# Two mixture-of-experts blocks: each up-projection from the third expert on as three products of high and low parts

## The reference

```
# layer 0: 8 routed experts, top 2, and one shared expert (a ninth with weight 1)
h = gelu(einsum('bsd,edi->bsei', x, ew1) + eb1)          # 128 -> 512
all_outputs = einsum('bsei,eid->bsed', h, ew2) + eb2     # 512 -> 128
moe_out = einsum('bse,bsed->bsd', weights_E, all_outputs)
# layer 1: 8 experts, top 2, each on its own scaled and shifted rows
normed = xhat[None] * gamma[:, None, :] + beta[:, None, :]
h = relu(einsum('end,edf->enf', normed, W1) + b1[:, None, :])
out = einsum('enf,efd->end', h, W2) + b2[:, None, :] + xf[None]
y = einsum('ne,end->nd', cw, out)
```

## Time and profile before

| | us |
|---|---|
| median of 3 runs | 4264.62 (4262.81 to 4272.31) |
| the profiled execution's own time | 4266.36 |
| its span | 4264.6 |
| PE busy | 4034.6 (95%) |
| DVE busy | 2708.3 (64%) |
| ACT busy | 1815.7 (43%) |
| POOL busy | 2786.1 (65%) |
| one up-projection of an expert on PE | 6.87 |
| one down-projection | 7.14 |

### The profile page before, as it was taken

How to read it: one execution, slowest core, us unless ns; L and a number is a source line. 1 busy time by engine, 2 the same in 40 slices (tenths; PEclk the granted TensorE clock), 3 DMA queues, 4 the chain that set the end, 5 groups by cost and what they waited for, 6 DMA issues and landing times. The chain is left out here.

```text
span 4264.6 us, 71858 instructions
## 1 busy us (share of the span) xinstructions
PE 4034.6 (95%) x26436; PEld 2145.7 (50%) x26436; DVE 2708.3 (64%) x3398; ACT 1815.7 (43%) x2105; POOL 2786.1 (65%) x1342
## 2 busy tenths in 40 slices
PE   7999799999999999999999998899799999999989
PEld 3444355555545545555555545533355554555547
DVE  5666867667676676766767743378667666676542
ACT  3444244444444444444444443246344444444433
POOL 4667087878887787877878891000078878878940
PEclk9999799999999999999999998869899999999989
DMA  1000000000000000000000001100000000000001
GB/s 36 7 6 2 5 2 2 2 2 2 3 2 3 2 2 2 2 3 2 2 1 1 2 1 28 35 1 1 5 2 2 2 2 2 2 1 2 1 13 33
DMA packets 25454, 23.92 MB, mean 6 GB/s; under 512 B 6321, under 2 KB 19106, under 8 KB 25122
## 3 DMA queue, kind: packets, MB, share of 16 engines
q1 hardware_dynamic: 23666, 17.05, 1.4%
q10 hardware_dynamic: 1456, 2.46, 0.2%
HBM read 18.97 MB, written 0.52 MB: 5 GB/s over the span
## 5 line engine op out<-in xcount | busy, mean ns | idle before, releaser
L421 POOL TENSOR_TENSOR c_SUM<-c_SUM,c_PR 128x896 f32<-128x896 f32 (+2 forms) x1170 | 2449.0, 2093 | 463.2 <-ACT c_PR L492 371.4
L588 DVE TENSOR_REDUCE c_MX<-c_XB 128x2 f32<-128x1024 f32 (+2 forms) x1156 | 1391.6, 1204 | 858.5 <-PE c_XB L788 858.3
L492 ACT ACTIVATE c_PR<-c_S 128x1024 f32<-128x1024 f32 (+1 forms) x1224 | 1195.1, 1023 | 1622.9 <-PE c_S L823 1547.2
L841 PE MATMUL c_O<-c_PR,c_V 128*64 128x512 f32 (+1 forms) x4896 | 1179.6, 600 | 0.0
L841 PEld LDWEIGHTS c_O<-c_PR,c_V 128*64 128x64 f32 (+1 forms) x4896 | 317.2, 136 | 540.8 <-issue 418.4
L823 PE MATMUL c_S<-c_SH,c_ONE 64*128 64x512 f32 x2448 | 490.8, 395 | 0.0
L788 PE MATMUL c_XB<-c_KHM,c_QH 64*128 64x512 f32 x1632 | 373.2, 452 | 29.1 <-DVE c_MX L588 20.6
L788 PEld LDWEIGHTS c_XB<-c_KHM,c_QH 64*128 64x128 f32 x1632 | 157.2, 188 | 389.3 <-DVE c_MX L588 211.7
L823 PE MATMUL c_S<-c_QH,c_KHM 64*128 64x512 f32 x1728 | 352.4, 403 | 0.3 <-DVE c_SH L578 0.3
L823 PE MATMUL c_S<-c_QL,c_KHM 64*128 64x512 f32 x1728 | 349.6, 398 | 0.0
L823 PE MATMUL c_S<-c_QH,c_KLM 64*128 64x512 f32 x1728 | 347.6, 397 | 0.0
(11 more groups left out here) (298 smaller groups left out, 4569.4 us busy)
## 6 DMA issues: line engine op xcount, KB each, us to landing
f_W<-in_L_w SPq DMA_DIRECT2D x34, 256.0 KB, 2.7
CTX<-in_ctx ACTq DMA_DIRECT2D x12, 192.0 KB, 4.4
c_WQ<-in_L_xattn_Wq SPq DMA_DIRECT2D x12, 64.0 KB, 1.8
c_WO<-in_L_xattn_Wo SPq DMA_DIRECT2D x12, 64.0 KB, 1.8
c_WK<-in_L_xattn_Wk SPq DMA_DIRECT2D x12, 48.0 KB, 1.7
c_WV<-in_L_xattn_Wv SPq DMA_DIRECT2D x12, 48.0 KB, 1.7
X<-in_x SPq DMA_DIRECT2D x1, 512.0 KB, 6.7
a_WQ<-in_L_attn_Wq SPq DMA_DIRECT2D x8, 64.0 KB, 1.9
```

Of the source, the lines that this page charges most:

```text
L421: pool.tensor_tensor(out[0:kp], out[0:kp], tile[0:kp], ALU.add).then_inc(summed, 1)
L492: act.activation(PR[0:kp, u % BUFS, :, :].rearrange("p h q -> p (h q)"), S[u % 2][0:kp, :], ACT.Exp)\
L588: dve.tensor_reduce(MX[:, q:q + tiles, :, column], bank[:].rearrange("p (h k) -> p h k", h=2) [:, :, 0:tiles * m].rearrange("p h (q k) -> ...
L841: last = pe.matmul(O[ROWS[h], :], V[pair.par][0:kp, t, ROWS[h]], PR[0:kp, u % BUFS, h, :], start=t == 0, stop=t == TILES - 1)
```

## The change

From the third expert of a block on (`e >= 2`; seven experts in `f0`, six in `f1`), `up` makes each unit out of three float32r matmuls that add up in the same bank: high weights by high rows, low weights by high rows, high weights by low rows. The product of the two low parts is left out. ScalarE makes the high parts (`W1H` of each expert's weights; `XEH` of its rows, once for the block in `f0`), VectorE the low parts (`W1L`, `XEL`). The first two experts keep the float32 matmul. Loads and `down` stay as they are.

```diff
+        W1H, W1L = [[sb(f"W1{part}{i}", [P, F], F32R) for i in range(2)] for part in "HL"]
+        several = 2 if normed is not None else 1
+        XEH, XEL = [[sb(f"XE{part}{i}", [P, N], F32R) for i in range(several)] for part in "HL"]
...
                 def up(e, par, ep):
-                    pe.wait_ge(w1_in[par], PER_W * (ep + 1))
-                    if normed is not None:
-                        pe.wait_ge(xe_done, e + 1)
+                    plain = isinstance(e, int) and e < 2
...
+                        terms = [(W1[par], XE[par])]
+                    else:
+                        xh, xl, made = parts(e, par)
+                        pe.wait_ge(w_low, e - 1)
+                        pe.wait_ge(x_low, made)
+                        terms = [(W1H[par], xh), (W1L[par], xh), (W1H[par], xl)]
...
-                            pe.matmul(UP[j % 4][:], W1[par][:, k * P:(k + 1) * P],
-                                      XE[par][:, half * 512:(half + 1) * 512], start=True, stop=True)\
-                              .then_inc(up_done, 1)
+                            for i, (stat, rows) in enumerate(terms):
+                                last = pe.matmul(UP[j % 4][:], stat[:, k * P:(k + 1) * P],
+                                                 rows[:, half * 512:(half + 1) * 512], start=i == 0, stop=i == len(terms) - 1)
+                            last.then_inc(up_done, 1)
...
+                def high_rows(e, par):
...
+                    act.activation(xh[:], XE[par][:], ACT.Copy).then_inc(x_high, 1)
...
+                    act.activation(W1H[par][:], W1[par][:], ACT.Copy).then_inc(w_high, 1)
...
+                    dve.tensor_tensor(xl[:], XE[par][:], xh[:].bitcast(F32), ALU.subtract).then_inc(x_low, 1)
...
+                    dve.tensor_tensor(W1L[par][:], W1[par][:], W1H[par][:].bitcast(F32), ALU.subtract).then_inc(w_low, 1)
...
                 def body(e, par, ep):
                     if normed is not None:
                         affine(e + 2, par, ep + 1)
+                        low_rows(e + 2, par)
+                    low_weights(e + 2, par)
                     add(e, par, ep)
```

More of the change, by code:

```diff
@@ L1418, in experts @@
             sem(n) for n in ("up_done", "h_done", "dn_done", "acc_done", "xe_done", "x_done")]
+        x_high, x_low, w_high, w_low = [sem(n) for n in ("x_high", "x_low", "w_high", "w_low")]
         PER_W = 16 * (3 if normed is not None else 2)
@@ L1427, in loop, with parts @@
                 body(e, e % 2, e // 2)
+        def parts(e, par):
+            return (XEH[par], XEL[par], e - 1) if normed is not None else (XEH[0], XEL[0], 1)
         def load_up(sp, e, par):
@@ L1474, in up @@
                 def up(e, par, ep):
-                    pe.wait_ge(w1_in[par], PER_W * (ep + 1))
-                    if normed is not None:
-                        pe.wait_ge(xe_done, e + 1)
+                    plain = isinstance(e, int) and e < 2
+                    if plain:
+                        pe.wait_ge(w1_in[par], PER_W * (ep + 1))
+                        if normed is not None:
+                            pe.wait_ge(xe_done, e + 1)
+                        terms = [(W1[par], XE[par])]
[4 more added lines that the diff above has]
+                        terms = [(W1H[par], xh), (W1L[par], xh), (W1H[par], xl)]
                     for k in range(KF):
@@ L1545, in _, with high_weights, body @@
                 act.activation(WT[0:count, 512:1024], DN[3][0:count, :], ACT.Copy).then_inc(wt, 1)
-                loop(act, lambda e, par, ep: hidden(e + 2, par, ep + 1))
+                def high_rows(e, par):
+                    xh, _, _ = parts(e, par)
+                    if normed is not None:
+                        act.wait_ge(xe_done, e + 1)
+                        act.wait_ge(up_done, 8 * e - 8)
+                    act.activation(xh[:], XE[par][:], ACT.Copy).then_inc(x_high, 1)
+                def high_weights(e, par, ep):
+                    act.wait_ge(w1_in[par], PER_W * (ep + 1))
+                    act.wait_ge(up_done, 8 * e - 8)
+                    act.activation(W1H[par][:], W1[par][:], ACT.Copy).then_inc(w_high, 1)
+                if normed is None:
+                    high_rows(2, 0)
+                def body(e, par, ep):
+                    if normed is not None:
+                        high_rows(e + 2, par)
+                    high_weights(e + 2, par, ep + 1)
+                    hidden(e + 2, par, ep + 1)
+                loop(act, body)
             @block.vector
@@ L1654, in add, with low_rows, low_weights @@
                         last.then_inc(acc_done, 1)
+                def low_rows(e, par):
+                    xh, xl, made = parts(e, par)
+                    dve.wait_ge(x_high, made)
+                    dve.tensor_tensor(xl[:], XE[par][:], xh[:].bitcast(F32), ALU.subtract).then_inc(x_low, 1)
+                def low_weights(e, par):
+                    dve.wait_ge(w_high, e - 1)
+                    dve.tensor_tensor(W1L[par][:], W1[par][:], W1H[par][:].bitcast(F32), ALU.subtract).then_inc(w_low, 1)
+                if normed is None:
+                    low_rows(2, 0)
                 def body(e, par, ep):
```

## The result

| | us |
|---|---|
| changed kernel, median of 4 runs | 4234.09 (4231.13 to 4243.71) |
| kernel before, median of its runs by then | 4268.47 (4262.81 to 4273.66) |
| ratio, 95% interval | 0.993 (0.9911 to 0.995) |
| the changed kernel's profiled execution, own time and span | 4231.13, 4228.3 |

The forecast was 4252.9 us with a range of 4243 to 4263. It was right that the kernel gets faster and wrong on how much: the time lies 9 us under the range.

A forecast was written before the change was run, and what follows sets the result against it. TensorE alone was taken to bound the expert loops. Each of 13 `up` was to fall from 6.87 to 5.97 us (5.62 + 0.35), 11.7 us in all: 4264.62 - 11.7 = 4252.9 us, range 4243 to 4263.

The forecast's parts named there:

- What bounds the kernel: Expert loops of `f0` and `f1`: TensorE alone is the chain, so time taken from an `up` (6.87 us) shortens the program.
- ScalarE and VectorE hidden: Expert loops: making high and low parts ends by 9.8 us, under `down`, with 3.3 us to spare before TensorE needs them.
- 24 x 0.234 us: Each changed `up`: 24 float32r matmuls at 0.234 us, read from pairs of 64 partitions in `c_S`, make 5.62 us.
- Two changes of type, 0.35 us: Each changed expert: switching into float32r and back to float32 for `down` adds 0.35 us together, read from cross-attention rows.
- cheaper pass: Changed `up`: float32r matmul at half a float32 record, type-change cost partly absent; 17 to 22 us less, 4242 to 4248; chance 0.15.
- Exposed weight loads: Changed `up`: every weight load shows, 0.34 us a matmul; 18.6 us more in all, 4283 us; chance 0.07.
- The clock elsewhere: Half-clock stretches behind the shortened block, as in `a1`, may shift; 8.5 us either way, 4261 or 4244; chance 0.11.

The follow-up runs named there:

- e10: Changed kernel with the float32r up-projections over the first 64 of 128 partitions alone, for timing only; 4265.4 us in one run.
- e11: Kernel before with the float32 up-projections from the third expert on over the first 64 partitions alone, for timing only; 4269.56 us in one run.
- e3: Kernel before with two empty lines more; median 4263.68 us, ratio 0.999 to before.
- e5: Kernel before with one more copy of `f0`'s result (0.7 us on VectorE) ahead of `a1`; 4258.73 us, ratio 0.9982.
- e8: Changed kernel with four more copies of `f0`'s result on VectorE ahead of `a1`; 4257.8 us in one run.
- e9: Changed kernel with matmuls that nobody reads put into TensorE's gaps in `a1`'s first part; 4257.99 us, ratio 0.9988.

## Why the prediction was wrong

- **What bounds the kernel**: right. The `up` of the loops stand on the chain, and the 1.41 us of each appear in full.
- **ScalarE and VectorE hidden**: right. In the changed kernel's timeline of one expert the last low part is done at 4161.3, 9.2 us behind the `up`'s start at 4152.1 (forecast 9.8), and TensorE wants it at 4164.7; durations as forecast:

```profile
4158.43 1.05 ACT L1569 ACTIVATE f_XEH<-f_XE 128x1024 fp32r<-128x1024 f32 x1
4159.37 0.62 ACT L1574 ACTIVATE f_W1H<-f_W 128x512 fp32r<-128x512 f32 x1
4159.51 1.23 DVE L1698 TENSOR_TENSOR f_XEL<-f_XE,f_XEH 128x1024 fp32r<-128x1024 f32 x1 [1.78 <-ACT f_XEH L1569]
4160.65 0.68 DVE L1702 TENSOR_TENSOR f_W1L<-f_W,f_W1H 128x512 fp32r<-128x512 f32 x1
```

- **24 x 0.234 us**: 0.227 measured at full height, 0.17 us an `up` too much. The pair of `c_S` is a little slower than one matmul alone, which takes 0.228 us over 64 partitions (e10). The Trainium skill's 215.7 ns ("TensorE: Matmul & The Clock Gate", Part 2) is not reached either.
- **Two changes of type, 0.35 us**: this step of the sum failed. In the earlier trace rows the cross-attention changes the tile's shape at the same places, and I put the price on the type. e10 and e11 give the shape 0.4 us with and without a change of type; the change itself pays some 0.01 us. With both terms mended the gain of an `up` is 1.41, not 0.90, and 18.3 us in all, not 11.7, which makes 4246.3. That is the time of the "cheaper pass" rival, and half of its mechanism: the cost of the change of type is absent, but a pass takes 0.227 us and not half a float32 record, 0.2145.
- **Exposed weight loads**: did not happen; each load runs under the matmul before it, in the same rows of the array (a load of 0.19 us, matmuls 0.227 us apart). The Trainium skill ("TensorE: Matmul & The Clock Gate", Part 3, "What overlaps and what doesn't") disagrees with this, as with `down` before.
- **The clock elsewhere**: this step failed too, and it put the time out of the range; with 4246.3 alone it would lie inside. The sum had this term at nothing, and I named the right place, `a1`, but held the effect for a coin without direction, of 8.5 us and 0.11 in chance. Measured, the clock gave 17.8 us (with the 18.3 of the `up`, 36.1 of the 36.3 us by which the span is shorter). 11.0 are `a1`'s: its main part takes 215 to 234 us by where it begins against the fall of the clock, and a shorter `f0` moves that place. For one program the place came out alike in two or three traces, so the gain repeats. But its direction was luck: nothing in the rows of before could tell that the new place would be the best one seen. The other 6.8 us are four short falls of the clock fewer in the second cross-attention. Its length was 1101 us in before, e3 and e5, 1100 in e8 and e10, and 1091 to 1097 in all others. What sets the number of these falls stays open, and not each microsecond at half clock costs half of it: e8 has 90.3 of them in that stage, 40 more than the changed kernel, and is 5.9 us longer.

## What to carry to other kernels

A float32 matmul of 512 columns (0.859 us) as three float32r products (0.68 us) pays where the matmuls are the chain, two other engines have idle time to make the parts, and the result can do without the product of the two low parts. Before a cost is read from a place where the kind of matmul changes, look whether the tile's shape changes there too. And where a stage sits at half clock for part of its length, a change far ahead of it can move it by as much as the change itself is worth (11.0 us against the 10.4 of `f0`): compare stages, not totals. Put a small delay ahead of the stage and read from the trace where it then begins, to see which part of a gain is luck of place.

## What the runs showed of the hardware

- Matmuls of 512 columns in float32r begin 0.227 us apart at 2.4 GHz over 128 partitions (the changed kernel) and 0.228 over 64 (e10).
- Two changes between tiles of 64 and of 128 partitions cost 0.39 us in float32 (e11) and 0.41 us where float32r takes turns with float32 (e10); two changes between these types at one shape cost 0.01 us (the changed kernel).
- In `a1` TensorE stayed at half clock while it was busy for 33.41 of 34.10 us (e9), and in e8 for 102.4 us, of the last 76.9 of which it was busy for 74.01. Once back, the clock fell again 6.9 us later (e9), in which TensorE was busy for 5.28 us. The Trainium skill ("TensorE: Matmul & The Clock Gate", Part 1) has the clock follow how busy the engine has been; by busy time as the profile counts it, these runs disagree.
